# Attention over 64 groups of heads: first scores issued behind the second scores, two inversions and the output's addition reordered, constants made inside the first router

## The chip, the cores and the metric

One core of a Trainium2 chip runs the whole program in one launch. Its engines work side by side and meet at semaphores: TensorE (PE; its weight loads are shown as PEld), VectorE (DVE), ScalarE (ACT), GpSimd (POOL), and SyncE (SP), which issues most DMAs. The metric is the device time of one launch in microseconds (us).

## The reference, cut to what matters

Layers in a row, each with a layer norm ahead and a residual addition behind: a mixture of experts (a router, 64 experts, 8 chosen for each token, at most 128 tokens each), the gated linear attention that this change is about, a second mixture of experts, and a closing stage. The attention, per head (16 sequences of 256 tokens, 16 heads, 64 key, 64 slot and 128 value channels):

```
s = clip(x @ Ws, -32, 32);  z = cumlogsumexp(s over time)
g = exp(z shifted by one - z);  p = exp(s - z)
ok_t = q_t . hk_t     with hk_t = hk_(t-1) * g_t + k_t p_t       (first scan)
pv   = softmax(ok)
ov_t = pv_t . hv_t    with hv_t = hv_(t-1) * g_t + p_t v_t       (second scan)
out  = (rmsnorm(ov) * silu(x @ Wg)) @ Wo
```

## The kernel before

The program is a row of stages: router and experts (0 to about 325 us), attention (to about 1790 us), router and experts again, closing. Before the first router two short stages stand: `constants` lets GpSimd make the identity, the causal mask and a few index tables, and `attention_weights` lets SyncE issue two small loads. Each such stage ends in a meeting of all engines, and only then does the router's SyncE issue the loads of x.

**The scans as matrices.** Both scans are turned into masked matrix products over the 256 tokens (two tiles of 128). With e = exp(s) (`em`) and its running sum over time (`running_sum`, then `invert`, giving `rz` = 1/sum), the first scan is: scores k.q of tokens j <= t (`scores_a`), masked (`masked_first`, into `at`), times e (`slots_read`, into PSUM bank `psC[0]`), times `rz` (`okn`). The softmax weights times `rz` are `pzT`. The second scan is: scores e.pz (`scores_b`), masked (`masked_second`, into `bt`), times v (`over_j`, into `psD`), plus for the second tile the state of the first (`state_of_slots`, copied by ScalarE to `state`, read by `state_read`).

**Rounds.** Attention is a software pipeline of 64 rounds, N = 16 sequences x 4 groups of 4 heads (`QPB` = 4). In round n TensorE finishes group n and projects group n+1. Its order is written out by hand in the last loop of `attention`: value(n+1, first half), slots_read(n), state_of_slots(n), slots(n+1), turn_back(n), value(n+1, second half), query(n+1), turn_weights(n), turn_exps(n+1), turn_output(n-1), key(n+1), scores_b(n), state_read(n), gate(n+1) twice, over_j(n), output(n-1), scores_a(n+1). VectorE and ScalarE have orders of their own. In every fourth round a new sequence's normalised x is turned (`turn_stream`) between the two gates, and copied in two parts by ScalarE (`high_of_stream`) and VectorE (`low_of_stream`).

**Names in the rows.** A projection is three matmuls for each part (lines 1460 to 1462 of `split_matmul`). L1292 is scores_b, L1304 state_read, L1268 and L1271 are scores_a (256 and 128 columns), L1316 slots_read, L1279 state_of_slots, L1325 turn_back. Key and slot channels are 64, so the scores use half of the array's rows: the trace shows them as 64*128, two heads side by side, while projections are 128*128 and slots_read and state_of_slots are 128*64. Float32 products are two records for each matmul. On VectorE L1092 is masked_second, L1086 masked_first, L1109 the running sums, L1113 the inversions, L1102 the gated output, L1098 the gate, L1076 the output's addition, L1117 the squares, L1139 okn.

**PSUM.** `psA[0]` and `psA[1]` take turns for all projections. `first_banks` are the four banks into which scores_a writes: both of `psB`, `psC[1]` and one of `psD`. So scores_a has to wait until the masks, the exps' copy, the gated output and the squares have read these banks.

Of the kernel before, what the change touches and what calls it, by code (L numbers as in the profile page):

```python
# [17 lines left out]
ALU = mybir.AluOpType  # L18
# [19 lines left out]
EPS = 1e-5  # L38
ROW = D + E
# [53 lines left out]
def constants(nc, mem):  # L93
# [14 lines left out]
    with nc.Block(no_gpsimd_drain=True) as block:  # L108
        @block.gpsimd
        def _(pool):  # L110
            nc.gpsimd.memset(c["ident"][:, :], 0.0).then_inc(s_set, 1)
            nc.gpsimd.memset(c["causal"][:, :, :], 1.0).then_inc(s_set, 1)
            nc.gpsimd.memset(c["minus_half"][:, :], -0.5).then_inc(s_set, 1)
            pool.wait_ge(s_set, 3)
            nc.gpsimd.affine_select(out=c["ident"][:, :], in_=c["ident"][:, :], compare_op=ALU.not_equal,
                                    fill=1.0, base=0, pattern=[[-1, P]], channel_multiplier=1).then_inc(s_cut, 1)
            for blk in (0, 2):
                nc.gpsimd.affine_select(out=c["causal"][:, blk, :], in_=c["causal"][:, blk, :],
                                        compare_op=ALU.is_ge, fill=0.0, base=0, pattern=[[1, P]],
                                        channel_multiplier=-1).then_inc(s_cut, 1)  # L120
            nc.gpsimd.memset(c["earlier"][:, :], 0.0).then_inc(s_blocks, 1)
            pool.wait_ge(s_blocks, 1)
            for k in range(4):
                own = slice(32 * k, 32 * k + 32)
                nc.gpsimd.memset(c["earlier"][own, own], 1.0).then_inc(s_blocks, 1)
                nc.gpsimd.iota(base_i[own, :], pattern=[[0, 1]], base=1, channel_multiplier=P).then_inc(s_iota, 1)
            pool.wait_ge(s_blocks, 5)
            pool.wait_ge(s_iota, 4)
            nc.gpsimd.iota(row_i[:, :], pattern=[[1, P]], base=0, channel_multiplier=0).then_inc(s_iota, 1)
            nc.gpsimd.iota(col_i[:, :], pattern=[[0, 1]], base=0, channel_multiplier=1).then_inc(s_iota, 1)  # L130
            nc.gpsimd.affine_select(out=c["earlier"][:, :], in_=c["earlier"][:, :], compare_op=ALU.is_ge, fill=0.0,
                                    base=-1, pattern=[[1, P]], channel_multiplier=-1).then_inc(s_cut, 1)
            pool.wait_ge(s_iota, 6)
            nc.gpsimd.tensor_copy(c["slot_row"][:, :], row_i[:, :]).then_inc(s_cut, 1)
            nc.gpsimd.tensor_copy(c["slot_col"][:, :], col_i[:, :]).then_inc(s_cut, 1)
            nc.gpsimd.tensor_copy(c["tile_base"][:, :], base_i[:, :]).then_inc(s_cut, 1)
            pool.wait_ge(s_cut, 7)
            nc.gpsimd.tensor_scalar(c["slot_half"][:, :], c["slot_col"][:, :], 0.5, None, ALU.add).then_inc(s_cut, 1)
            nc.gpsimd.tensor_scalar(c["slot_pad"][:, :], c["slot_col"][:, :], float(NTOK - P + 1), None, ALU.add).then_inc(s_cut, 1)
            pool.wait_ge(s_cut, 9)  # L140
    return c


def moe_router(nc, cst, tag, past, x_src, gate_w, rows, fresh, slot_tok, behind=()):
# [10 lines left out]
    with ExitStack() as ctx:  # L155
# [79 lines left out]
        with nc.Block(no_gpsimd_drain=True) as block:  # L235
            @block.sync
            def _(sp):
# [16 lines left out]
                for j in range(1, NJ):  # L254
                    load(j)
                if fresh:
# [19 lines left out]
            def _(act):  # L276
# [14 lines left out]

                act.wait_ge(gw_turned, DC)
# [62 lines left out]
            def _(dve):  # L355
# [32 lines left out]

                for j in range(S):
                    moments_of(j)  # L390
# [57 lines left out]
            def _(pe):  # L448
# [25 lines left out]

                pe.wait_ge(gw_here, 16)
# [283 lines left out]
def attention_weights(nc, mem, g_norm, lut):  # L759


    w = {"norm": mem.sb("g_norm", [P, 1]), "lut": mem.sb("lut_row", [P, NLUT]), "here": mem.sem("attention_weights")}
    with nc.Block(no_gpsimd_drain=True) as block:
        @block.sync
        def _(sp):
            with nc.allow_non_contiguous_dma(reason="128 words, once"):
                sp.dma_start(w["norm"][:, :], g_norm.rearrange("(v o) -> v o", o=1)).then_inc(w["here"], 16)
            sp.dma_start(w["lut"][:, :], lut.partition_broadcast(P)).then_inc(w["here"], 16)
    return w


def attention(nc, cst, w, tag, past, stream_a, stream_b, x_out, second, zero_row, indices, looked_up):
# [10 lines left out]
    with ExitStack() as ctx:  # L783
# [16 lines left out]
        at = mem.sb("at", [P, HQ, 3 * P])  # L800
        bt = at.rearrange("p h i -> p (h i)")[:, 0:HQ * T].rearrange("p (q s i) -> p q s i", q=2, i=P)
        state = at.rearrange("p h i -> p (h i)")[:, HQ * T:HQ * T + NH * DV].rearrange("p (a v) -> p a v", a=NH)
        sq = mem.sb("sq", [P, TT * HQ * DV])
        okn = sq[:, 0:NH * T].rearrange("p (a t) -> p a t", a=NH)
# [18 lines left out]
        psO = [psD[:, k, :] for k in range(2)]  # L823
        first_banks = psB + [psC[1], psO[0]]
# [31 lines left out]
        with nc.Block(no_gpsimd_drain=True) as block:  # L856
# [186 lines left out]
            def _(dve):  # L1043
# [85 lines left out]
                for a in range(NH):  # L1129
                    invert(0, a)  # L1130
# [957 lines left out]
```

## Time and profile before

| | us |
|---|---|
| median of 3 runs | 2640.36 (2638.11 to 2642.53) |
| the profiled execution | 2640.57 |
| its span, first to last instruction | 2638.4 |
| TensorE busy | 2341.7 (89%) |
| VectorE busy | 1736.6 (66%) |
| GpSimd busy | 1241.8 (47%) |
| ScalarE busy | 886.0 (34%) |
| DMA, mean rate over the span | 63 GB/s |

By slices of the span, TensorE is 90% busy or more from about 400 us to 1780 us and again from 2200 us on: the attention and the closing stage. In the two router and expert stages it is 40 to 80% busy and the DMA engines carry 150 to 275 GB/s. The granted TensorE clock is full through attention and falls to half in stretches of the router and expert stages. A busy share says how full an engine is, not who is waited for: for that, the timeline of one round is read engine by engine.

### The profile page before, as it was taken

What the parts mean: (1) busy time and instruction counts of PE and PEld (TensorE: products, weight loads), DVE (VectorE), ACT (ScalarE), POOL (GpSimd) and SP (SyncE); (2) the same over time, 40 slices, a digit from 0 to 9 for tenths busy, and PEclk for the clock granted to TensorE, in tenths of its full rate; (3) what the DMA queues carried; (4) which work ended last, traced back from release to release, by engine and by line L of the source; (5) the groups of instructions that cost most, each with busy time, mean ns of one, the idle gap of its engine ahead of it and who ended that gap; (6) DMA issues with size and microseconds to landing.
All of it is one profiled execution on the core that took longest, in us unless ns stands there. A gap on an engine that the chain in (4) does not pass through costs nothing. (4 is left out here: it accounts for less than half of the span.)

```text
span 2638.4 us, 46098 instructions
## 1 busy us (share of the span) xinstructions
PE 2341.7 (89%) x18006; PEld 2076.9 (79%) x18006; DVE 1736.6 (66%) x3420; ACT 886.0 (34%) x1768; POOL 1241.8 (47%) x1214
## 2 busy tenths in 40 slices
PE   7656499999999999999999999987566489999998
PEld 7545388889899888989998889877554377888887
DVE  6433267888787788777887887766422266776654
ACT  5322133333333333333333333324322133333332
POOL 3477634555455555545554555452488521221111
PEclk9788799999999999999999999988799799999999
DMA  8989500000000000000000000004799500000000
GB/s 275 274 224 216 115 13 21 5 17 22 9 17 17 21 6 19 19 21 5 17 21 21 6 17 21 13 3 153 207 218 215 120 24 17 25 25 25 17 9 16
DMA packets 188230, 165.43 MB, mean 63 GB/s; under 512 B 28432, under 2 KB 180976, under 8 KB 187504
## 3 DMA queue, kind: packets, MB, share of 16 engines
q1 hardware_dynamic: 161072, 120.53, 14.9%
q0 software_dynamic: 24576, 37.77, 7.8%
q10 hardware_dynamic: 2368, 4.19, 0.5%
q8 instruction: 145, 2.38, 0.4%
q14 instruction: 69, 0.57, 0.1%
HBM read 115.84 MB, written 51.04 MB: 63 GB/s over the span
## 5 line engine op out<-in xcount | busy, mean ns | idle before, releaser
L947 POOL TENSOR_TENSOR a_orstd<-a_ms,minus_half 128x8 f32<-128x8 f32 x64 | 106.7, 1667 | 467.6 <-DVE a_ms L1120 467.6
L927 POOL TENSOR_SCALAR a_pick<-a_index,lut_row 128x258 f32<-128x258 int32 x240 | 280.8, 1170 | 24.3
L1113 DVE RECIPROCAL a_rz<-a_rz 128x256 f32<-128x256 f32 x128 | 215.6, 1716 | 0.0
L630 PE MATMUL e_psX<-ident,e_xg 128*128 128x128 f32 x256 | 61.7, 327 | 167.3 <-DMA e_xg<-rows,slot_tok 166.7
L746 DVE TENSOR_TENSOR e_hT<-e_psH,e_sil 128x128 f32<-128x128 f32 x128 | 37.2, 291 | 256.5 <-ACT e_sil L704 151.7
L630 PEld LDWEIGHTS e_psX<-ident,e_xg 128*128 128x128 f32 x256 | 30.7, 156 | 211.9 <-DMA e_xg<-rows,slot_tok 208.6
L930 POOL TENSOR_TENSOR a_found<-a_found,a_pick 128x258 f32<-128x258 f32 x240 | 177.4, 739 | 20.0
L600 POOL DMA_INDIRECT e_xg<-rows,slot_tok x128 | 129.9, 1015 | 93.5 <-POOLq L235 55.1
L958 ACT ACTIVATE a_v<-a_psA 128x512 f32<-128x512 f32 x128 | 76.5, 598 | 224.1 <-PE a_psA L1462 224.1
L1460 PE MATMUL a_psC<-wo_high,a_oT 128*128 128x256 f32 x512 | 150.2, 293 | 1.5 <-DVE a_oT L1066 1.5
L1460 PE MATMUL f_pair<-f_lnT,wguT 128*128 128x512 f32 (+1 forms) x352 | 143.7, 408 | 7.5 <-DVE f_lnT L1726 7.2
L1461 PE MATMUL a_psC<-wo_low,a_oT 128*128 128x256 f32 x512 | 144.6, 282 | 0.0
L1462 PE MATMUL a_psC<-wo_high,a_oT 128*128 128x256 f32 x512 | 144.4, 282 | 0.0
L1737 DVE TENSOR_TENSOR f_hs<-f_pair,f_sil 128x512 f32<-128x512 f32 x96 | 66.1, 689 | 117.0 <-PE f_pair L1462 106.8
L1461 PE MATMUL f_pair<-f_lnT,wguT 128*128 128x512 f32 (+1 forms) x352 | 140.9, 400 | 0.0
L1462 PE MATMUL f_pair<-f_lnT,wguT 128*128 128x512 f32 (+1 forms) x352 | 140.6, 400 | 0.0
L952 POOL TENSOR_TENSOR a_o<-a_o,a_orstd 128x512 f32<-128x512 f32 x128 | 131.0, 1044 | 5.0
L1036 ACT ACTIVATE a_sq<-a_psD 128x512 f32<-128x512 f32 x128 | 76.6, 598 | 165.0 <-DVE a_o L1102 98.0
L1343 PEld LDWEIGHTS a_psD<-a_v,a_at 128*128 128x128 f32 x1024 | 124.2, 192 | 5.9 <-DVE a_at L1092 0.2
L1634 ACT ACTIVATE f_sil<-f_pair 128x512 f32<-128x512 f32 x96 | 57.2, 597 | 211.0 <-PE f_pair L1462 211.0
L688 ACT ACTIVATE e_xgT<-e_psX 128x256 f32<-128x256 f32 x128 | 49.0, 383 | 232.0 <-PE e_psX L630 195.6
L1092 DVE TENSOR_TENSOR a_at<-a_psB,causal 128x512 f32<-128x512 f32 x128 | 82.5, 686 | 65.2 <-PE a_psB L1292 65.2
(279 smaller groups left out, 7857.3 us busy)
## 6 DMA issues: line engine op xcount, KB each, us to landing
e_wg<-in_L_ffn_w_gate SPq DMA_DIRECT2D x128, 128.0 KB
e_wu<-in_L_ffn_w_up SPq DMA_DIRECT2D x128, 128.0 KB
e_wd<-in_L_ffn_w_down SPq DMA_DIRECT2D x128, 128.0 KB
rows<-r_row SPq DMA_DIRECT2D x32, 320.0 KB, 2.8
stream_b<-r_zeros SPq DMA_DIRECT2D x11, 384.0 KB, 4.9
stream_c<-rows SPq DMA_DIRECT2D x33, 128.0 KB, 3.2
r_xt<-in_L_attn_hidden_states SPq DMA_DIRECT2D x16, 256.0 KB, 5.6
stream_a<-r_xt SPq DMA_DIRECT2D x16, 256.0 KB, 3.6
```

Of the source, the lines that this page charges most:

```text
L600: pool.indirect_dma_start(out=xg[:, e % U, :], out_offset=None, in_=rows, in_offset=bass.IndirectOffsetOnAxis(ap=slot_tok[:, e:e + 1], axi ...
L630: nc.tensor.transpose(psX[u][:, c, :], xg[:, e % U, c * P:(c + 1) * P], cst["ident"][:, :]).then_inc(turned[u], 1)
L927: nc.gpsimd.tensor_scalar(pick[:, :, :], index[:, :, :], float(c), w["lut"][:, c:c + 1], ALU.is_equal, ALU.mult).then_inc(picked, 1)
L930: nc.gpsimd.tensor_tensor(out=found[:, :, :], in0=found[:, :, :], in1=pick[:, :, :], op=ALU.add).then_inc(looked, 1)
L947: nc.gpsimd.tensor_tensor(out=flat(orstd[:, :, :]), in0=ms[:, :], in1=cst["minus_half"][:, 0:TT * HQ], op=ALU.pow).then_inc(orstd_ok, 1)
L952: nc.gpsimd.tensor_tensor(out=part, in0=part, in1=orstd[:, :, 2 * a:2 * a + 2].unsqueeze(3).to_broadcast([P, TT, 2, DV]), op=ALU.mult).the ...
L1092: nc.vector.tensor_tensor(out=bt[:, p, :, :], in0=psB[p].rearrange("p (s i) -> p s i", i=P), in1=cst["causal"][:, 0, :].unsqueeze(1).to_br ...
L1113: nc.vector.reciprocal(rz[:, a, :], rz[:, a, :]).then_inc(rz_ok, 1)
L1343: mm = nc.tensor.matmul(psD[:, p, (t * NH + a) * DV:(t * NH + a + 1) * DV], bt[:, p, a * TT + t, :], v[:, n % 2, t, h * DV:(h + 1) * DV], ...
L1460: nc.tensor.matmul(out, lhs[0], rhs[0], start=first, stop=False)
L1461: nc.tensor.matmul(out, lhs[0], rhs[1], start=False, stop=False)
L1462: return nc.tensor.matmul(out, lhs[1], rhs[0], start=False, stop=last)
```

## The change

**Scores.** scores_a is split. `own_scores`, shared with scores_b, makes the products of each token tile with itself (8 matmuls of 128 columns, into the two `psA` banks that query and key have just left), and `scores_below` makes those of the first tile with the second (4 matmuls of 128 columns, into the first half of `psD`). The below part needs no mask: ScalarE copies it (`below_copy`, two copies of 128x256) into a new tile `below`, whose first half is `state` at other times. VectorE masks the own part with two operations of 128x512 instead of four of 128x384. `bt` now lies in `sq`. All of it stands right behind scores_b(n). The first projection of value(n+1) now comes behind slots_read and state_of_slots, output(n-1) comes ahead of over_j, the gates behind it. The gates wait for the masks of the first scores. `turn_stream` writes `psB[1]`, and low_of_stream comes behind the gates on VectorE. over_j signals once, not once for each bank, and waits for the below copies.

```diff
-                def masked_first(m):
-                    for h in range(HQ):
-                        dve.wait_ge(at_ps, HQ * m + h + 1)
-                        nc.vector.tensor_tensor(out=at[:, h, :], in0=first_banks[h][:, 0:3 * P],
...
+                def masked_first(m):
+                    masked(at, [psA[1 - m % 2], psA[m % 2]], m, at_ps, at_ok)
...
+                def below_copy(m):
+                    act.wait_ge(below_ps, m + 1)
+                    for p in range(2):
+                        copy(flat(below[:, p, :, :]), psD[:, p, 0:NH * P], below_ok)
...
                 def gate(m, t):
-                    if t == 0:
-                        pe.wait_ge(q_ok, m + 1)
-                    else:
-                        pe.wait_ge(k_ok, m + 1)
+                    pe.wait_ge(at_ok, 2 * m + t + 1)
...
                 def scores_a(m):
                     pe.wait_ge(k_ok, m + 1)
                     pe.wait_ge(q_ok, m + 1)
-                    pe.wait_ge(et_ok, m + 1)
-                    if m > 0:
-                        pe.wait_ge(bt_ok, 2 * m)
...
+                    own_scores(kT, qT, [psA[1 - m % 2], psA[m % 2]], at_ps)
+
+                def scores_below(m):
+                    if m > 1:
+                        pe.wait_ge(otl_ok, NH * (m - 1))
...
                 def slots_read(n):
+                    pe.wait_ge(at_ok, 2 * n + 2)
+                    pe.wait_ge(below_ok, 2 * n + 2)
...
                 def over_j(n):
+                    if n + 1 < N:
+                        pe.wait_ge(below_ok, 2 * n + 4)
```

On TensorE, in a third round, this stands in a row where scores_a was and where it is now (the names are output<-inputs; a_ stands for attention). Before:

```order
L1462 MATMUL a_psC<-wo_high,a_oT 128x256
L1268 MATMUL a_psB<-a_qT,a_kT 128x256 x2
L1271 MATMUL a_psB<-a_qT,a_kT 128x128 x2
L1268 MATMUL a_psC<-a_qT,a_kT 128x256
L1268 MATMUL a_psD<-a_qT,a_kT 128x256
L1271 MATMUL a_psC<-a_qT,a_kT 128x128
L1271 MATMUL a_psD<-a_qT,a_kT 128x128
L1460 MATMUL a_psA<-wv_high,a_lnT 128x512
```

Now, behind the last matmul of key and ahead of the first of output:

```order
L1479 MATMUL a_psA<-a_lnT,wk_low 128x256
L1269 MATMUL a_psB<-a_pzT,a_emT 128x128 x8
L1269 MATMUL a_psA<-a_qT,a_kT 128x128 x8
L1287 MATMUL a_psD<-a_qT,a_kT 128x128 x4
L1315 MATMUL a_psD<-a_below,a_pzT 128x128 x4
L1477 MATMUL a_psC<-wo_high,a_oT 128x256
```

All products of 64 channels are one run, and between two runs of that shape no projection is left in which they would have to be set up again.

**VectorE's order.** masked_first(n+1) moves right behind masked_second(n), the inversions stay behind the sums, and add_output(n-1) moves from behind the gates to between the two inversions. Before, on VectorE in the same round:

```order
L1092 TENSOR_TENSOR a_at<-a_psB,causal 128x512 x2
L1109 SCALAR_TENSOR_TENSOR a_rz<-causal,a_psC 128x256 x2
L1113 RECIPROCAL a_rz<-a_rz 128x256 x2
L1102 TENSOR_TENSOR a_o<-a_psD,a_tg 128x4x128 x2
L1098 SCALAR_TENSOR_TENSOR a_tg<-a_tg,a_psA 128x512 x2
L1076 TENSOR_TENSOR a_xacc<-a_psC,a_xacc 128x512
L1086 TENSOR_TENSOR a_at<-a_psB,causal 128x384 x2
L1086 TENSOR_TENSOR a_at<-a_psC,causal 128x384
L1086 TENSOR_TENSOR a_at<-a_psD,causal 128x384
L1117 TENSOR_REDUCE a_ss<-a_sq 128x8
```

Now:

```order
L1097 TENSOR_TENSOR a_sq<-a_psB,causal 128x512 x2
L1097 TENSOR_TENSOR a_at<-a_psA,causal 128x512 x2
L1120 SCALAR_TENSOR_TENSOR a_rz<-causal,a_psC 128x256 x2
L1124 RECIPROCAL a_rz<-a_rz 128x256
L1087 TENSOR_TENSOR a_xacc<-a_psC,a_xacc 128x512
L1124 RECIPROCAL a_rz<-a_rz 128x256
L1113 TENSOR_TENSOR a_o<-a_psD,a_tg 128x4x128 x2
L1109 SCALAR_TENSOR_TENSOR a_tg<-a_tg,a_psA 128x512 x2
L1128 TENSOR_REDUCE a_ss<-a_sq 128x8
```

The mask of the first scores has left the place ahead of the squares; the same holds ahead of the first round, with one difference, that there the two inversions stand ahead of the mask.

**Start.** The stage `constants` is gone: its GpSimd work runs at the head of the router's GpSimd program, and VectorE, ScalarE and TensorE wait there for its nine last operations. The stage `attention_weights` is gone: SyncE issues its two loads behind the 16 loads of x.

```diff
+def moe_router(nc, cst, tag, past, x_src, gate_w, rows, fresh, slot_tok, behind=(), make=None, late=()):
...
                 for j in range(1, NJ):
                     load(j)
+                for dst, src, here in late:
...
+                act.wait_ge(cst["made"], MADE)
...
                 past.clear(pool)
+                if make:
+                    make(pool)
...
+                dve.wait_ge(cst["made"], MADE)
                 for j in range(S):
                     moments_of(j)
...
+                pe.wait_ge(cst["made"], MADE)
                 pe.wait_ge(gw_here, 16)
```

SyncE's program began before with:

```order
L764 UNCONDITIONAL_BRANCH
L767 DMA g_norm<-in_L_attn_g_norm_weight 128x1
L768 DMA lut_row<-in_L_ffn_lut 128x16
L763 UNCONDITIONAL_BRANCH
L236 UNCONDITIONAL_BRANCH
L240 DMA r_xt<-in_L_attn_hidden_states 128x2x256 x2
```

and begins now with:

```order
L238 UNCONDITIONAL_BRANCH
L242 DMA r_xt<-in_L_attn_hidden_states 128x2x256 x2
L255 DMA r_gw_in<-in_L_ffn_gate_w 64x256
L242 DMA r_xt<-in_L_attn_hidden_states 128x2x256 x14
L260 DMA g_norm<-in_L_attn_g_norm_weight 128x1
L260 DMA lut_row<-in_L_ffn_lut 128x16
```

The loads of x are now the first thing on SyncE, with no meeting of the engines ahead of them.

## Rows read from the trace of the kernel before

**Rows 1.** Windows, the attention stage: busy us of each engine, then TensorE's clock share.

```profile
327.00:1780.00 1453.00, 1438.73 (x12324) 1295.06 (x12324) 1146.42 (x1769) 515.56 (x912) 754.58 (x747) 0.99 0.05 15
```

**Rows 2.** Timeline, PE, round at 1004 us: start us, us, line, operation, shape, count.

```profile
1003.84 1.16 PE L1292 MATMUL a_psB<-a_pzT,a_emT 64*128 64x128 f32 x16
1004.83 0.61 PE L1304 MATMUL a_psD<-a_at,a_pzT 64*128 64x128 f32 x8
...
1012.68 0.28 PE L1461 MATMUL a_psC<-wo_low,a_oT 128*128 128x256 f32 x1
1012.79 0.28 PE L1462 MATMUL a_psC<-wo_high,a_oT 128*128 128x256 f32 x1
1013.00 0.70 PE L1268 MATMUL a_psB<-a_qT,a_kT 64*128 64x256 f32 x4
...
1013.98 0.38 PE L1268 MATMUL a_psC<-a_qT,a_kT 64*128 64x256 f32 x1
...
1014.19 0.27 PE L1271 MATMUL a_psC<-a_qT,a_kT 64*128 64x128 f32 x1
...
1014.30 0.27 PE L1271 MATMUL a_psC<-a_qT,a_kT 64*128 64x128 f32 x1
...
1014.51 0.51 PE L1460 MATMUL a_psA<-wv_high,a_lnT 128*128 128x512 f32 x1
1014.85 0.40 PE L1461 MATMUL a_psA<-wv_low,a_lnT 128*128 128x512 f32 x1
1015.09 0.40 PE L1462 MATMUL a_psA<-wv_high,a_lnT 128*128 128x512 f32 x1
...
1019.54 0.60 PE L1325 MATMUL a_psC<-ident,a_sq 128*128 128x128 f32 x4
...
1026.07 1.16 PE L1292 MATMUL a_psB<-a_pzT,a_emT 64*128 64x128 f32 x16
```

**Rows 3.** Timeline, PE, the same operation at the end of a fourth round.

```profile
1049.08 1.16 PE L1292 MATMUL a_psB<-a_pzT,a_emT 64*128 64x128 f32 x16
```

**Rows 4.** Timeline, DVE, the same round.

```profile
1005.03 1.29 DVE L1092 TENSOR_TENSOR a_at<-a_psB,causal 128x512 f32<-128x512 f32 x2 [0.94 <-PE a_psB L1292]
...
1014.35 1.01 DVE L1086 TENSOR_TENSOR a_at<-a_psB,causal 128x384 f32<-128x384 f32 x2
...
1016.21 1.21 DVE L1117 TENSOR_REDUCE a_ss<-a_sq 128x8 f32<-128x1024 f32 x1
...
1017.69 0.69 DVE L1139 TENSOR_TENSOR a_sq<-a_psC,a_rz 128x512 f32<-128x512 f32 x1
```

**Rows 5.** Timeline, ACT, the same round: the copy of the keys.

```profile
1003.94 0.60 ACT L958 ACTIVATE a_kT<-a_psA 128x512 f32<-128x512 f32 x1 [0.78 <-PE a_psA L1462]
```

**Rows 6.** Timeline, all engines, the start of the program.

```profile
5.23 0.21 POOL L139 TENSOR_SCALAR slot_pad<-slot_col 128x1 f32<-128x1 f32 x1
...
7.20 0.89 SPq L240 DMA_DIRECT2D r_xt<-in_L_attn_hidden_states  x2
...
10.77 1.41 DVE L361 BATCH_NORM_STATS2 r_bs<-r_xt 128x6 f32<-128x256 f32 x4 [10.77 <-DMA r_xt<-in_L_attn_hidden_states]
...
14.03 1.40 DVE L361 BATCH_NORM_STATS2 r_bs<-r_xt 128x6 f32<-128x256 f32 x4 [1.44 <-DMA r_xt<-in_L_attn_hidden_states]
```

**Rows 7.** Timeline, all engines, ahead of attention's first round.

```profile
339.32 3.34 DVE L1113 RECIPROCAL a_rz<-a_rz 128x256 f32<-128x256 f32 x2
...
344.93 1.66 PE L1316 MATMUL a_psC<-a_at,a_em 128*64 128x128 f32 x24
```

**Rows 8.** Timeline, PE, in the first experts: a wait of 2.66 us.

```profile
227.62 0.64 PE L630 MATMUL e_psX<-ident,e_xg 128*128 128x128 f32 x2 [2.66 <-DMA e_xg<-rows,slot_tok]
```

**Rows 9.** Windows, right behind that wait (columns as in Rows 1).

```profile
227.80:231.00 3.20, 3.20 (x14) 2.78 (x14) 0.43 (x2) 1.38 (x3) 2.59 (x3) 0.50 0.89 182
```

**Rows 10.** Timeline, DVE, attention's last round.

```profile
1769.08 1.29 DVE L1102 TENSOR_TENSOR a_o<-a_psD,a_tg 128x512 f32<-128x512 f32 x2 [1.66 <-PE a_psD L1343]
...
1772.54 1.21 DVE L1117 TENSOR_REDUCE a_ss<-a_sq 128x8 f32<-128x1024 f32 x1
```

More of the change, by code:

```diff
@@ L38 @@
 EPS = 1e-5
+MADE = 9
 ROW = D + E
@@ L107, in constants @@
     s_set, s_cut, s_blocks, s_iota = mem.sem("c_set"), mem.sem("c_cut"), mem.sem("c_blocks"), mem.sem("c_iota")
[L108 to L140, printed above, removed]
@@ L1253, in turn_exps, with own_scores @@
                     mm.then_inc(et_ps, 1)
+                def own_scores(lhs, rhs, banks, ready):
+                    for a in range(NH):
+                        for t in range(TT):
+                            for p in range(2):
+                                r, own = p * DK, slice(t * P, (t + 1) * P)
+                                mm = nc.tensor.matmul(banks[p][:, (a * TT + t) * P:(a * TT + t + 1) * P], lhs[r:r + DK, a, own], rhs[r:r + DK, a, own],
+                                                      start=True, stop=True)
+                                if a == NH - 1 and t == TT - 1:
+                                    mm.then_inc(ready, 1)
                 def scores_a(m):
@@ L1287, in scores_b, with state_read @@
                     pe.wait_ge(st_ok, n + 1)
[L1288 to L1297 removed]
+                    pe.wait_ge(lnTl_ok, n // QPB + 1)
+                    own_scores(emT, pzT, psB, bt_ps)
+                def state_read(n, more):
                     if n > 0:
@@ L1371, in _ @@
                 turn_exps(0)
+                scores_a(0)
+                scores_below(0)
                 gate(0, 0)
                 gate(0, 1)
-                scores_a(0)
                 for n in range(N):
                     ahead = n + 1 < N
-                    if ahead:
-                        value(n + 1, 0)
                     slots_read(n)
@@ L1394, in _ @@
                     scores_b(n)
-                    state_read(n)
+                    if ahead:
+                        scores_a(n + 1)
+                        scores_below(n + 1)
+                    state_read(n, ahead)
+                    if n > 0:
+                        output(n - 1)
+                    over_j(n)
                     if ahead:
@@ L1400, in _ @@
                         gate(n + 1, 1)
-                    over_j(n)
-                    if n > 0:
-                        pe.wait_ge(lnTl_ok, min((n + 1) // QPB + (2 if (n + 1) % QPB == QPB - 1 else 1), B))
-                        output(n - 1)
-                    if ahead:
-                        scores_a(n + 1)
                 turn_output(N - 1)
```

149 lines of the change are left out of this document (84 added, 65 removed).

## The prediction

> **What bounds the kernel now.** I read the page by slices first: the attention stage is more than half of the span, and TensorE is full in it. The windows view puts a number on it: of 1453 us of attention TensorE works 1438.73 at full clock (0.99), VectorE 1146, ScalarE 516, GpSimd 755 [rows 1]. So a round costs what TensorE's row of matmuls costs, and a change pays if it shortens that row. The timeline of TensorE through one round is next. The round from one scores_b to the next is 1026.07 - 1003.84 = 22.23 us, a fourth round 1049.08 - 1026.07 = 23.01 us [rows 2, 3]. Inside it TensorE is never without work, but steps between matmuls are not even: output's matmuls follow each other in 0.12 us, the last one holds 0.21 before scores_a starts (1012.79 to 1013.00); within scores_a a pass of two heads takes 0.21 for 256 columns (1013.98 to 1014.19) and 0.11 for 128 (1014.19 to 1014.30), but its last pass of 128 again holds 0.21 (1014.30 to 1014.51); value's first matmul then takes 0.34 where the next takes 0.24 [rows 2]. The longer steps stand where the shape changes from 128*128 to 64*128 and back. That is what the change takes out.
>
> **The round's matmuls, part by part.** scores_a takes 1014.51 - 1013.00 = 1.51 us [rows 2]. Its columns alone are four passes of 256 and four of 128 for pairs of heads: 4 x 0.215 + 4 x 0.107 = 1.29 us. Moved into the run behind scores_b, it is eight passes of 128 (own) and four (below), 12 x 0.107 = 1.29 us again: the columns are the same. state_read follows scores_b today with no long step between them (16 records, 1003.84 to 1004.83, 0.99 us, are eight passes and one step of 0.11-0.14 at the run's start) [rows 2], so I price the joints inside the new run at nothing. What goes: 1.51 - 1.29 = 0.22 in scores_a, 0.21 - 0.12 = 0.09 ahead of it, 0.34 - 0.24 = 0.10 behind it: 0.41 us. The other shape changes stay in number: the run ends into output instead of the gate, the gate instead of value goes into slots_read (128*64), state_of_slots goes into value instead of slots. Six changes become four, and I take 0.40 us a round. Bounds: 0.19, if the 0.22 inside scores_a belongs to its waits and not to the shape, and 0.50, if a pair's start is also saved.
>
> The change has 12 matmuls where 8 stood. The row shows no price for that: half the columns take half the time, 0.11 against 0.21 [rows 2]. The Trainium skill (TensorEngine Tiling, Instruction Overhead) gives each matmul about 60 cycles of overhead; by it, as an estimate, four more matmuls of two passes at 2.4 GHz would cost 0.2 us a round and leave half of the gain, 12 us less in all. The row decides for no price.
>
> 62 of the 63 rounds that look ahead gain this: 62 x 0.40 = 24.8 us.
>
> **Which waits could take it back.** In the new order, counted from scores_b's start: scores_a needs the keys' copy. ScalarE begins it at 1003.94 and ends it 0.70 behind scores_b's start [rows 2, 5], scores_a is due at 0.99: 0.3 to spare. Its banks psA are left by then. scores_below (due at 1.85) needs low_of_output, which was ready for state_read. The run ends at 2.83. Output has no new wait. over_j needs the below copies: ScalarE can start them at 2.9; a copy of 128x512 is 0.60 [rows 5], so two of half the size are at most 1.2, done by 4.1; over_j is due behind output's 24 matmuls, at 5.75. The gates (7.45) need the masks, done at about 3.7. Queued behind ScalarE's below copies are turned_exps and the squares, due later still.
>
> VectorE is the engine to watch, since okn and turn_back hang on it. Today it goes from masked_second (1005.03) to okn (1017.69) in 12.66 us [rows 4]. The four masks of 128x384 there take 1016.21 - 1014.35 = 1.86; two masks of 128x512 take what masked_second takes, about 1.21. Everything else is the same work in another order. So okn starts 12.0 us behind masked_second, at 1.19 + 12.0 = 13.2, and is done at 13.9. turn_back stands today at 1019.54 - 1003.84 = 15.70 [rows 2], and would stand at 15.3. VectorE is 1.4 us ahead. The addition between the inversions waits for output (ended at 5.8), the second inversion ends at 8.6, over_j's single signal comes at 7.7: no wait. GpSimd's output scaling starts with the squares, 0.5 earlier than today, like its user. Earlier stores of the addition only help the next sequence's accumulator.
>
> In the fourth rounds value(n+2) waits for low_of_stream, which now stands behind the gate on VectorE: ScalarE's second tanh 11.6, high part 12.1, low part 12.95, value due at 12.8: 0.2 to 0.3 us of wait. Today these rounds cost 0.78 more than others [rows 2, 3], of which the turn is 0.43 (four transposes, 0.36, and a step of 0.07 at the gate behind them); new: 0.43 + 0.27 = 0.70. 15 x 0.08 = 1.2, I take 1.0 us gained.
>
> **Ahead of the first round** the change loses. VectorE inverts twice before it masks: the inversions run from 339.32 to 342.6 [rows 7]. The gates now wait for these masks (343.3), where they filled this time before; TensorE, whose new scores are done 1.4 us behind the keys' copy, near 339.8, stands until 343.3, 3.5 us. Then gates (3.0) and slots_read at 346.3, where it was at 344.93 [rows 7], and value(1) (1.5) still follows: 1.4 + 1.5 = 2.9, less 0.1 for a shape step: 2.8 us lost. A pause of 2.66 us in the experts was followed by 3.2 us at half clock (0.50) [rows 8, 9]; that would cost 1.7 here. It need not happen; I take 1.0, bounds 0 and 3.4.
>
> **Behind the last round** output(62) now runs ahead of over_j(63). The gated output moves from 1769.08 to about 1771.9; then square and second part, and the squares' sum starts near 1773.0 instead of 1772.54 [rows 10]: 0.5 lost. The last turn before it waits for VectorE and gains about the 0.5 of okn: together nothing.
>
> **Start.** GpSimd's constants end at 5.44 and are not touched in length; the loads of x are issued at 7.20, and VectorE starts on them at 10.77, 3.57 later; on the second batch at 14.03 [rows 6]. In the new order SyncE issues them as its first work, which I put at 0.8 (the constants' own stage, about 4.6 us long, cannot have begun later than that), so they are there at 4.4, and VectorE starts when the constants are made, 5.5: 5.3 earlier. The second batch is there at 7.6, 6.4 earlier. What follows hangs on both, and all later stages shift with it; the two late small loads add 0.8 us to SyncE ahead of its zero stores, which nobody waits for. I take 6.0, bounds 4 (part of it swallowed by busy DMA engines in the experts) and 6.4.
>
> **Sum** against the profiled execution, 2640.57, which is the median (2640.36) within 0.2: - 24.8 (rounds) - 1.0 (fourth rounds) + 2.8 + 1.0 (before the first) + 0 (end) - 6.0 (start) = - 28.0, 2612.6; I say 2612.
>
> **Rivals.**
> A, part of the joint is not saved: the long steps are scores_a's own waits, and the joint of scores_b and scores_a, with new operands and a wait on the keys' copy 0.3 us away, costs as much again. Then 0.19 a round, 62 x 0.21 = 13 us less: 2625. For it: two semaphores stand ahead of scores_a; against it, state_read follows scores_b without a step, though it waits too.
> B, slower: the loop over VectorE becomes the bound. Its work from masked_second to okn is in series with turn_back, two projections, the exps and scores_b. It has 1.4 us to spare of the new round, so 1.4 + 0.40 = 1.8 us against today's. It turns slower only where the new order puts more than 1.9 us of waits into VectorE's row, as if over_j's one late signal, the two tanh and the inversions fell in series instead of overlapping. At 2.1 us: 63 x 0.3 = 19 us slower than now, with - 6 + 3.8 at the edges, 2657. The ends worked out above speak against it: the signal comes 0.9 ahead of its reader.
> C, the start saves nothing, because the DMA-bound experts set the time: 2618; inside the range.
> D, the waits of several tenths spread over the round eat the gain just so far that nothing is measured: 2640.
>
> **How the numbers follow.** Forecast (2603 to 2621, C's case within) 0.77; A (to 2632) 0.13; lower than 2603, a larger saving at the joints, 0.03; B 0.05; D 0.02. A measurement of this kernel can tell about 0.2%, 5 us, from no change. Faster 0.93, same 0.02, slower 0.05. The range takes the bounds of the start (2 us), of the clock (2.4) and a good part of A: 2602 to 2628.
>
> **What would show it.** TensorE's timeline: L1269, L1269, L1287, L1315 in one run of about 2.83 us, and rounds of 21.84 (fourth rounds 22.5). The first x statistics at 5.5 us. One new wait of TensorE of about 3.5 us at the first gates, in the first round a short wait of over_j and value. If the round is 22.0 or more, the waits of TensorE name which semaphore; if it is PEld that starts late at the second L1269, it is A. If VectorE's okn ends behind the last slots matmul, it is B.

## The result

| | before | after |
|---|---|---|
| median of 4 runs, us | 2641.23 (2638.11 to 2642.53) | 2611.10 (2609.42 to 2613.99) |
| the profiled execution, us | 2640.57 | 2609.42 |
| its span, us | 2638.4 | 2607.7 |

The ratio is 0.9892, with a 95% interval of 0.9880 to 0.9903: 28.5 us faster by the ratio, 30.8 by the two profiled spans. The forecast was 2612.

The page of the changed kernel: span, then busy us of each engine with its share and instructions.

```profile
span 2607.7 us, 47039 instructions
PE 2317.5 (89%) x18518; PEld 2077.7 (80%) x18518; DVE 1691.2 (65%) x3292; ACT 927.1 (36%) x1896; POOL 1241.8 (48%) x1214
```

TensorE is busy 24 us less, in the same share of the span, and ScalarE 41 us more, which are the below copies. Attention by windows, as in [rows 1]: TensorE is still full and its clock still whole.

```profile
311.00:1750.00 1439.00, 1414.37 (x12840) 1294.15 (x12840) 1102.45 (x1646) 556.58 (x1041) 760.09 (x752) 0.99 0.06 15
```

**The round.** TensorE's timeline, over the same operations as [rows 2, 3]: the end of key, the joined run, the start of output, and scores_b one round before and one and two rounds later.

```profile
987.97 0.38 PE L1269 MATMUL a_psB<-a_pzT,a_emT 64*128 64x128 f32 x2
...
1009.64 0.28 PE L1479 MATMUL a_psA<-a_lnT,wk_low 128*128 128x256 f32 x1
1009.85 1.16 PE L1269 MATMUL a_psB<-a_pzT,a_emT 64*128 64x128 f32 x16
1010.85 1.06 PE L1269 MATMUL a_psA<-a_qT,a_kT 64*128 64x128 f32 x16
1011.74 0.61 PE L1287 MATMUL a_psD<-a_qT,a_kT 64*128 64x128 f32 x8
1012.19 0.61 PE L1315 MATMUL a_psD<-a_below,a_pzT 64*128 64x128 f32 x8
1012.73 0.38 PE L1477 MATMUL a_psC<-wo_high,a_oT 128*128 128x256 f32 x1
...
1032.41 1.16 PE L1269 MATMUL a_psB<-a_pzT,a_emT 64*128 64x128 f32 x16
...
1054.29 0.38 PE L1269 MATMUL a_psB<-a_pzT,a_emT 64*128 64x128 f32 x2
```

The four blocks of 64*128 follow each other with no wait: scores_b holds TensorE for 1010.85 - 1009.85 = 1.00 us, the own scores 0.89, the below scores 0.45, state_read 0.54 up to output. The run takes 2.88 us. Ordinary rounds are 1009.85 - 987.97 = 21.88 and 1054.29 - 1032.41 = 21.88 us long, where they were 22.23; the fourth round between them is 22.56, where it was 23.01.

**Where the 30.8 us are.** The same landmarks on both traces, by the start of TensorE's operation, and of VectorE's last addition for attention's last operation (us from the span's start; the gains are taken before rounding):

| landmark | before | after | gained in this piece |
|---|---|---|---|
| first matmul of the first expert | 88.8 | 83.8 | 5.1 |
| attention's first turn | 325.2 | 317.2 | 2.9 |
| first scores_b | 354.1 | 350.4 | -4.2 |
| scores_b of round 1 | 375.4 | 370.6 | 1.0 |
| scores_b of round 62 | 1744.0 | 1715.5 | 23.8 |
| last scores_b | 1764.0 | 1734.5 | 1.0 |
| attention's last operation | 1785.2 | 1756.6 | -0.9 |
| closing's first turn | 2098.2 | 2069.3 | 0.2 |
| end of the span | 2638.4 | 2607.7 | 1.9 |

Attention itself is 24 us of it, the start 5, and 3 + 2 us came in stages whose instructions are the same in both kernels. Of the 24.8 us from the first scores_b to that of round 62, round 0 gives 1.0 (21.21 us before, 20.18 now), the 61 rounds behind it 0.36 each (22.24 to 21.88 us in the mean of the 46 ordinary ones), and the 15 fourth rounds among these 1.9 more.

**Ahead of the first round** the forecast wait is there. All engines, with the wait in brackets:

```profile
330.28 3.34 DVE L1124 RECIPROCAL a_rz<-a_rz 128x256 f32<-128x256 f32 x2
...
333.54 1.22 DVE L1097 TENSOR_TENSOR a_at<-a_psA,causal 128x512 f32<-128x512 f32 x2
...
334.22 0.80 PE L1477 MATMUL a_psA<-wg_high,a_lnT 128*128 128x512 f32 x1 [3.30 <-DVE a_at L1097]
```

VectorE inverts from 330.28 to 333.5 and masks only then; TensorE's first gate stands 3.30 us for that mask. Behind it the windows view (busy us of PE, PEld, DVE, ACT, POOL, then the clock) shows TensorE at 0.50 for 6.4 us:

```profile
333.60:340.00 6.40, 5.78 (x16) 4.16 (x18) 1.85 (x4) 0.85 (x2) 0.00 (x0) 0.50 0.00 0
```

By narrower windows the stretch at half clock runs from 333.4 to 340.2. Against it stands the half-clock stretch of attention's own start, just before: 306.2 to 333.5 in the kernel before and 299.3 to 323.2 now. TensorE does nothing in it until the first turn; from there on it is 8.3 us in the kernel before (325.2 to 333.5) and 6.0 us now (317.2 to 323.2).

**VectorE in the round** goes through masks, sums, inversions and addition in one row, as [rows 4] did in another order:

```profile
1011.05 1.29 DVE L1097 TENSOR_TENSOR a_sq<-a_psB,causal 128x512 f32<-128x512 f32 x2 [1.03 <-PE a_psB L1269]
1012.25 1.28 DVE L1097 TENSOR_TENSOR a_at<-a_psA,causal 128x512 f32<-128x512 f32 x2
...
1014.62 1.73 DVE L1124 RECIPROCAL a_rz<-a_rz 128x256 f32<-128x256 f32 x1
...
1024.13 0.69 DVE L1150 TENSOR_TENSOR a_sq<-a_psC,a_rz 128x512 f32<-128x512 f32 x1
...
1025.89 0.60 PE L1340 MATMUL a_psC<-ident,a_sq 128*128 128x128 f32 x4
```

okn (L1150) ends at 1024.82 here, turn_back (L1340) starts 1.07 later, in this fourth round; in ordinary rounds it is 1.42, and 1.06 in some of those just ahead of a fourth round. The one wait of TensorE that is new inside the rounds, by the view of waits (what waited, for whom: us in total, times, longest us):

```profile
PE a_psA L1477 <- DVE a_lnT L1071: 2.6, 15, 0.2
```

That is value(n+2) waiting for low_of_stream, once in each of 15 fourth rounds.

**The start.** All engines; SPq is SyncE's issue:

```profile
0.79 0.94 SPq L242 DMA_DIRECT2D r_xt<-in_L_attn_hidden_states  x2
...
5.48 1.41 DVE L369 BATCH_NORM_STATS2 r_bs<-r_xt 128x6 f32<-128x256 f32 x4 [5.48 <-POOL slot_pad L139]
...
7.23 1.41 DVE L369 BATCH_NORM_STATS2 r_bs<-r_xt 128x6 f32<-128x256 f32 x4
```

The loads go out at 0.79 instead of 7.20, VectorE starts its statistics at 5.48 instead of 10.77, behind the last constant and no longer behind a DMA, and does the second batch at 7.23 instead of 14.03 [rows 6].

### The profile page after: what moved, and what is told of

It reads as the page before. It is cut to its first block and busy times, and to the rows that moved or that the text cites. A ratio compares the mean times of both kernels' runs of the same rounds, so it can differ in the third digit from the quotient of the medians.

```text
span 2607.7 us, 47039 instructions
## 1 busy us (share of the span) xinstructions
PE 2317.5 (89%) x18518; PEld 2077.7 (80%) x18518; DVE 1691.2 (65%) x3292; ACT 927.1 (36%) x1896; POOL 1241.8 (48%) x1214
## 5 line engine op out<-in xcount | busy, mean ns | idle before, releaser
L1124 DVE RECIPROCAL a_rz<-a_rz 128x256 f32<-128x256 f32 x128 | 221.4, 1731 | 0.0
L1109 DVE SCALAR_TENSOR_TENSOR a_tg<-a_tg,a_psA 128x512 f32<-128x512 f32 x128 | 87.9, 688 | 61.1 <-ACT a_tg L1005 55.3
L1360 PE MATMUL a_psD<-a_v,a_sq 128*128 128x128 f32 x1024 | 124.8, 275 | 0.8 <-ACT a_below L962 0.8
```

The source lines that it names most:

```text
L1109: nc.vector.scalar_tensor_tensor(out=tg[:, t, :], in0=tg[:, t, :], scalar=1.0, in1=psA[(1 - m % 2) if t == 0 else m % 2], op0=ALU.add, op1 ...
L1124: nc.vector.reciprocal(rz[:, a, :], rz[:, a, :]).then_inc(rz_ok, 1)
L1360: mm = nc.tensor.matmul(psD[:, p, (t * NH + a) * DV:(t * NH + a + 1) * DV], bt[:, p, a * TT + t, :], v[:, n % 2, t, h * DV:(h + 1) * DV], ...
```

## The experiments

The theories that they tell apart: a round gains by the two changes of array shape that are gone (the forecast), or by scores_a's waits that are gone (rival A); VectorE's loop has 1.2 to 1.4 us of room, and decides the sign beyond it (rival B); the earlier start reaches the end of the program or is swallowed by the DMA-bound experts (rival C). All ratios are against runs of the kernel before on the same chip.

### start_alone and attention_alone: the two parts apart

`start_alone` is the changed kernel with its whole `attention` as in the kernel before; in the row of a round:

```diff
-                    if ahead:
-                        scores_a(n + 1)
-                        scores_below(n + 1)
-                    state_read(n, ahead)
-                    if n > 0:
-                        output(n - 1)
-                    over_j(n)
+                    state_read(n)
...
+                    over_j(n)
...
+                        output(n - 1)
+                    if ahead:
+                        scores_a(n + 1)
```

> The kernel before with the start's part of the change alone (constants made at the head of the router, no stage for the two small loads). Theory: the first statistics start at 5.5 us instead of 10.8, the first experts' first matmul about 5 us earlier, and later stages shift along: 2635 (2633 to 2637). Rival C: the DMA-bound experts set the time and swallow it: 2641, with attention starting where it did, at 325 us.

Measured: 2630.51 us (2628.49 to 2632.20) against 2637.64 (2633.50 to 2639.61), ratio 0.9973 (0.9963 to 0.9984), 7.1 us faster. `attention_alone` is the other half, the kernel before with the changed `attention`, so the same lines the other way round:

> The kernel before with the attention's part of the change alone; constants and the two small loads stay in stages of their own. Theory: rounds - 24.8, ahead of the first round + 4.2, the end 0, as in the changed kernel's trace: about - 21 us, a ratio of 0.992 to the kernel before (2616 where before is 2637), and from the first experts' first matmul to attention's start between 233 and 238 us, wherever the start stands. If the experts' stage is 3 us shorter only when the program starts earlier, this kernel shows 236 and the others 233.

Measured: 2619.13 us (2613.68 to 2621.20) against 2639.44 (2635.88 to 2643.93), ratio 0.9917 (0.9898 to 0.9936), 22 us faster, with rounds of 21.88 us. The ratios multiply to 0.9890, the whole change has 0.9892: the parts add. Rival C has fallen.

The view of one tile (line, engine, tile and count: least, median and longest ns, from first to last us) gives the experts' first and attention's first matmul. Of start_alone, then of attention_alone:

```profile
L640 PE MATMUL e_psX<-ident,e_xg x128: 272/328/476, 82.5 to 290.0; 128*128 128x128 f32 x128
L1200 PE MATMUL a_psC<-ident,a_xab x4: 421/421/473, 315.6 to 316.3; 128*128 128x128 f32 x4
```

```profile
L630 PE MATMUL e_psX<-ident,e_xg x128: 272/328/476, 89.6 to 297.6; 128*128 128x128 f32 x128
L1201 PE MATMUL a_psB<-ident,a_xab x4: 421/421/476, 323.2 to 323.9; 128*128 128x128 f32 x4
```

The first matmul of the experts comes 6.3 us earlier with the new start (88.8 before) and 0.8 later without it. In the nine traces that have the new start it stands at 82.2 to 83.8, in the mean 83.1, in the two without it at 88.8 and 89.6: 6.1 us between the means. From there to attention it takes 315.6 - 82.5 = 233.1 with the new start and 323.2 - 89.6 = 233.6 without it, 236.3 in the trace of before, 233.5 in that of after, and 231.9 to 237.6 over all eleven traces of this study. So the 2.9 us that the experts gave on top are their scatter from one execution to another, not the change.

### turn_between and turn_behind: is it the shape?

Each adds one turn of the identity (128*128, into a bank that output is about to overwrite), the first inside the joined run, the second at its end, where the shape changes anyway. The work added is the same; only the first adds two shape changes.

```diff
                     scores_b(n)
+                    nc.tensor.transpose(psC[0][:, 0:P], ident, ident)
                     if ahead:
                         scores_a(n + 1)
```

```diff
                     state_read(n, ahead)
+                    nc.tensor.transpose(psC[0][:, 0:P], ident, ident)
```

> The same turn, but between scores_b and scores_a, so that the run of 64*128 products is cut in two. Nothing else moves and no wait is added. Theory (the saving is the change of shape): 0.09 for the turn and the 0.36 us a round that the change gained come back: 63 x 0.45 = 28 us over the changed kernel, 2639, scores_b's block grows by about 0.3 us and scores_a's by 0.1. Rival A (the saving lies in fewer or earlier waits): the same as the control, 2617.

> The changed kernel plus one turn of the identity (128*128, 128 columns) in each round, behind state_read and ahead of output, where the shape changes anyway. Both theories: 0.09 us a round for the turn itself and no new change of shape: 63 x 0.09 = 6 us, 2617. It is the control for the next kernel.

turn_between took 2637.55 us (2632.95 to 2640.07), ratio 1.0000 (0.9991 to 1.0010): the whole gain of attention and of the start is gone. turn_behind took 2612.81 (2609.80 to 2614.47), ratio 0.9901 (0.9884 to 0.9917), as the change itself. TensorE's timeline of turn_between:

```profile
1045.13 1.16 PE L1269 MATMUL a_psB<-a_pzT,a_emT 64*128 64x128 f32 x16
1046.22 0.33 PE L1412 MATMUL a_psC<-ident 128*128 128x128 f32 x1
1046.48 1.16 PE L1269 MATMUL a_psA<-a_qT,a_kT 64*128 64x128 f32 x16
1047.47 0.61 PE L1287 MATMUL a_psD<-a_qT,a_kT 64*128 64x128 f32 x8
```

and of turn_behind:

```profile
1015.59 0.61 PE L1287 MATMUL a_psD<-a_qT,a_kT 64*128 64x128 f32 x8
1016.03 0.61 PE L1315 MATMUL a_psD<-a_below,a_pzT 64*128 64x128 f32 x8
1016.58 0.33 PE L1416 MATMUL a_psC<-ident 128*128 128x128 f32 x1
1016.66 0.36 PE L1478 MATMUL a_psC<-wo_high,a_oT 128*128 128x256 f32 x1
```

In the run, scores_b holds TensorE for 1.09 us instead of 1.00, the turn for 1046.48 - 1046.22 = 0.26, the own scores for 0.99 instead of 0.89. At the end of the run the same turn holds 1016.66 - 1016.58 = 0.08, and output's first matmul is 0.05 shorter for it, since the change of shape is now paid ahead of it. Rounds are 22.30 and 21.91 us: the two shape changes cost 0.39 us, which over 63 rounds is the 24.7 us between the two medians. In both kernels the semaphores and their order are the same, so rival A's waits have no part in it. The Trainium skill (TensorEngine Tiling (Array Packing), Key Properties) says that a change of tiling mode drains TensorE; the 0.39 us agrees in kind, and the page gives no size.

### vector_sums_1 and vector_sums_2: how much room VectorE has

Behind masked_first(n+1) VectorE sums a tile that is ready, once or twice; nobody uses the result. The edit for two sums:

```diff
                         masked_first(n + 1)
+                        dve.wait_ge(tg_ok, TT * n + TT)
+                        if n > 0:
+                            dve.wait_ge(spared, 2 * n)
+                        for k in range(2):
+                            nc.vector.reduce_sum(spare[:, k:k + 1], flat(tg[:, :, :]), axis=AX.X).then_inc(spared, 1)
```

> The changed kernel with one more sum of 128x1024 (about 1.2 us, its result unused) in VectorE's row of each round, behind the masks of the first scores. Theory: VectorE is 1.4 us ahead at turn_back and 1.2 at value's first half, so the ordinary rounds do not move by more than 0.1 us; in the 15 fourth rounds, where TensorE waits for low_of_stream already, the whole 1.2 shows: 15 x 1.2 = 18 us over the changed kernel, up to 24: 2629 to 2635. If VectorE had no room (rival B nearly true), 62 x 1.2 = 74: 2685. If it had much more room than thought, 2611.

> The same with two such sums, 2.4 us. Theory: room of 1.2 us used up, so 1.2 in each of 48 ordinary rounds and 2.4 in 15 fourth rounds, 58 + 36 = 94 us over the changed kernel, 2705: slower than the kernel before, as rival B said for waits of over 1.9 us. If the room is nearer 2 us: 2640 to 2660.

VectorE's timeline of vector_sums_1 shows the sum behind the masks and the running sums behind it:

```profile
1013.71 1.28 DVE L1099 TENSOR_TENSOR a_at<-a_psA,causal 128x512 f32<-128x512 f32 x2
1014.90 1.21 DVE L1180 TENSOR_REDUCE a_spare<-a_tg 128x1 f32<-128x1024 f32 x1
1016.03 1.25 DVE L1122 TENSOR_TENSOR_SCAN a_rz<-causal,a_psC 128x256 f32<-128x256 f32 x2
```

It holds VectorE for 1016.03 - 1014.90 = 1.13 us. vector_sums_1 took 2622.92 us (2616.26 to 2625.48) against 2636.37 (2635.15 to 2649.14), ratio 0.9947 (0.9926 to 0.9968). Its ordinary rounds are 21.89 us in the mean, 0.01 longer than without the sum; its fourth rounds 23.03, 0.47 longer, and less than the 1.2 that I had expected. The view of waits has the reason: there TensorE waits for VectorE's low_of_stream, and in the changed kernel VectorE stands idle for 0.56 us ahead of the second gate, just before it, so part of the sum was covered.

```profile
PE a_psA L1484 <- DVE a_lnT L1073: 9.7, 15, 0.7
```

From the first to the last scores_b this kernel takes 10 us more than the change, where 18 to 24 were expected. By the two ratios (0.9947 and 0.9892) it is 14.5 us; the traced execution was the fastest of the four. vector_sums_2, one run, took 2696.18 us. Ordinary rounds are 23.03 us, longer by 1.15, as expected, fourth rounds 24.15. The view of waits, from 400 to 1700 us, has 42 rounds in which the first matmul of a projection waits for VectorE to leave its bank (a_tg is the gate's product), and the 14 fourth rounds as before:

```profile
PE a_psA L1484 <- DVE a_tg L1111: 46.0, 42, 1.1
PE a_psA L1484 <- DVE a_lnT L1073: 24.9, 14, 1.8
```

In ordinary rounds the first sum costs 0.01 us, and both cost 1.15, so the room is 2 x 1.13 - 1.15 = 1.1 us. That is a little less than the 1.4 that the prediction had read at turn_back: the gate's bank is due first (1.22 us to spare in the changed kernel's trace). With two sums the kernel is 60 us slower than the one before (2636.37). Rival B's mechanism is real, its point lies 0.3 us nearer than forecast, and the change doesn't reach it.

### addition_back: the output's addition behind the gates, as it was

```diff
                         invert(n + 1, 0)
-                    if n > 0:
-                        add_output(n - 1)
                     if ahead:
                         invert(n + 1, 1)
...
                             low_of_stream((n + 1) // QPB + 1)
+                    if n > 0:
+                        add_output(n - 1)
                     squares(n)
```

> The changed kernel with the output's addition back behind the gates on VectorE, where it stood before. slots_read of the next round waits for it, since both use the bank psC 0. It would be done about 12.5 us behind scores_b's start, and slots_read is due at 10.45: 2.1 us a round, 62 x 2.1 = 130 us over the changed kernel, 2741. Rival (the move of the addition was free, VectorE has room): 2611.

One run: 2767.97 us, where the kernel before takes 2636.37 on the same chip. From the first scores_b to that of round 62 it is 158 us more than the changed kernel. The timeline of PE and DVE in an ordinary round, and the view of waits:

```profile
1024.50 0.68 DVE L1087 TENSOR_TENSOR a_xacc<-a_psC,a_xacc 128x512 f32<-128x512 f32 x1
1025.24 0.44 PE L1331 MATMUL a_psC<-a_at,a_em 128*64 128x128 f32 x4 [2.07 <-DVE a_xacc L1087]
```

```profile
PE a_psC L1331 <- DVE a_xacc L1087: 131.1, 59, 2.7
```

slots_read writes the bank that the addition reads, so TensorE stands 2.07 us in each ordinary round and 2.67 in a fourth: the rounds are 24.0 and 25.05 us. In the kernel before, scores_a and value stood between the gates and slots_read and gave the addition its time; now only the gates and over_j lie between output and slots_read. So the joined run pays only with this move beside it. The 130 us that I expected are this wait. The rest is clock: in 14 of the 61 rounds from round 1 to 61 TensorE fell to half clock within 1.4 us behind the end of this wait, for 3.4 us each, and such a round is 1.6 us longer, 25.6 us if ordinary and 26.6 if a fourth; 14 x 1.6 = 22 us. Ten of the 14 are fourth rounds, with the wait of 2.67 us, of which there are 15; four are ordinary, with 2.07 us, of which there are 46. In vector_sums_2, where TensorE waits 1.8 us in a fourth round and 1.1 in an ordinary one, it is two of 15 and none of 46. So in these two kernels the half clock follows more often the longer the wait is. One such stretch and what follows it, by windows:

```profile
1099.80:1103.00 3.20, 3.20 (x15) 2.43 (x12) 0.69 (x1) 0.00 (x0) 3.12 (x3) 0.50 0.00 0
1103.20:1106.00 2.80, 2.80 (x22) 2.62 (x21) 1.07 (x2) 1.21 (x3) 2.52 (x4) 1.00 0.00 0
```

### mask_ahead and both_edges: the two ends mended

`mask_ahead` lets VectorE mask the first round's scores before it inverts:

```diff
+                masked_first(0)
                 for a in range(NH):
                     invert(0, a)
-                masked_first(0)
                 gate(0, 0)
```

> The changed kernel with the first scores' masks ahead of the two inversions on VectorE before round 0 only. Theory: TensorE's pause of 3.3 us at the first gates goes, and with it the stretch of half clock of 6.8 us that follows it (3 us): the first scores_b comes 5 to 6 us earlier, 2605 to 2606. If the half clock has another cause, 2608. Rival (okn's inversions then hold TensorE as long as the masks did): 2611.

It took 2606.11 us (2604.80 to 2608.76), ratio 0.9882 (0.9865 to 0.9898). PE and DVE:

```profile
331.65 1.29 DVE L1097 TENSOR_TENSOR a_at<-a_psA,causal 128x512 f32<-128x512 f32 x2
332.39 0.50 PE L1477 MATMUL a_psA<-wg_high,a_lnT 128*128 128x512 f32 x1 [0.33 <-DVE a_at L1097]
332.86 3.35 DVE L1124 RECIPROCAL a_rz<-a_rz 128x256 f32<-128x256 f32 x2
...
345.89 1.16 PE L1269 MATMUL a_psB<-a_pzT,a_emT 64*128 64x128 f32 x16
```

The wait of 3.30 us is 0.33, and the gates and what follows run at full clock, by windows:

```profile
331.00:340.00 9.00, 8.67 (x80) 7.22 (x77) 6.80 (x8) 3.22 (x7) 0.00 (x0) 1.00 0.01 2
```

From the first turn to the first scores_b it takes 28.7 us, as in the kernel before (29.0), where the change takes 33.1. The other traces agree: seven have the wait of 3.30 us, and a stretch of half clock begins within a microsecond of its end in all seven, 6.8 us long in two (the change and vector_sums_1) and 3.4 in five. The four without this wait have no such stretch.

`both_edges` has this, and in the last round over_j stands ahead of output again, and add_output(62) behind the gated output:

```diff
-                    if n > 0:
+                    if n > 0 and ahead:
                         add_output(n - 1)
...
                     gated_output(n, 0)
+                    if not ahead:
+                        add_output(n - 1)
...
                     state_read(n, ahead)
+                    if not ahead:
+                        over_j(n)
                     if n > 0:
                         output(n - 1)
-                    over_j(n)
+                    if ahead:
+                        over_j(n)
```

> The changed kernel with the masks of the first scores ahead of the two inversions before round 0, and, in the last round alone, over_j ahead of output and the output's addition behind the gated output, as they stood before the change. Theory: 4 to 5 us from the first, 0.5 to 0.9 us from the second: 0.9868 to 0.988 of the kernel before, 2605.5 on the chip of the first timing. If the last round's order costs nothing, the same as with the masks alone.

It took 2604.99 us (2602.79 to 2614.89) against 2636.37, ratio 0.9881 (0.9861 to 0.9901). From the last scores_b to the squares' means it takes 9.34 us instead of 9.91, so the order at the end is worth some 0.5 us in the trace. start_alone and attention_alone, the old order and the new, compare better, since neither has more than 0.1 us of half clock behind its last scores_b: 8.88 and 9.64 us, 0.76 between them. In the time it can't be seen. Both kernels come out ahead of the change (0.9892), but all three intervals overlap: a better version is likely, and not proven by the times. The 4.5 us in the trace of mask_ahead are the firmest part of it.

## Why the prediction was right

**The round.** Forecast 0.40 us, measured 0.36 in the mean of 46 ordinary rounds. The cause is the one named, two of six shape changes less: put back, they cost 0.39. The two steps inside scores_a, of which the text was not sure, stood at its ends, next to the other shape. The last is in [rows 2]; for the first, from the same timeline of the kernel before:

```profile
1013.00 0.70 PE L1268 MATMUL a_psB<-a_qT,a_kT 64*128 64x256 f32 x4
1013.54 0.39 PE L1271 MATMUL a_psB<-a_qT,a_kT 64*128 64x128 f32 x4
```

Two passes of 256 columns take 0.54 us here, where one alone takes 0.21 further on in [rows 2]: 0.11 too much.

What is missing is in the term for the new run, 2.83 us forecast and 2.88 measured. The twelve passes of the first scores take 0.89 + 0.45 = 1.34 us, 0.112 each, where I had 1.29 from 0.107 each. So a pass of 128 columns costs 0.004 more than half of one with 256 (0.216). The four matmuls more are 0.03 us of the 0.05; the rest is that the four passes of 128 that stood in scores_a before were put too low as well. The Trainium skill (TensorEngine Tiling (Array Packing), Instruction Overhead) puts about 60 cycles on each matmul, from which the prediction worked out an estimate of 0.2 us; the rows show 0.03. From the first scores_b to that of round 62, which are 62 rounds, the landmarks show 1.0 + 23.8 = 24.8 us gained; forecast for them, fourth rounds included, were 24.8 + 1.0 = 25.8.

**Fourth rounds.** In the mean of 15 their excess over an ordinary round was 0.81 us and is 0.68, where 0.70 was forecast, with the wait for low_of_stream at 0.17 us against 0.27. They give 15 x 0.13 = 1.9 us against 1.0. Round 0 gives 0.7 us more than an ordinary round, which was not in the sum. So a part of what the ordinary rounds lack came from terms that were put too low or not at all.

**The waits.** In ordinary rounds none of the limits that the text went through ends last. ScalarE copies the below scores late enough to be seen and early enough not to matter:

```profile
1009.96 0.60 ACT L962 ACTIVATE a_kT<-a_psA 128x512 f32<-128x512 f32 x1 [0.78 <-PE a_psA L1479]
...
1012.85 0.66 ACT L962 ACTIVATE a_below<-a_psD 128x256 f32<-128x256 f32 x2 [2.29 <-PE a_psD L1315]
```

The keys' copy starts 0.11 us behind scores_b and ends 0.29 ahead of the own scores, with 0.3 forecast. The below copies start 3.00 us behind scores_b (2.9 forecast). VectorE is 1.42 us ahead at turn_back, with 1.4 forecast; what was missed is that the gate's bank is due with less to spare, 1.2 (and turn_back itself with 1.06 in some rounds), and the sums show 1.1.

**Ahead of the first round.** Forecast +2.8 and +1.0 for the clock, measured +4.2, against +3.8; the pause is 3.30 against 3.5 us. The prediction said that the half clock need not happen and took 1.0 for it; it came in all seven traces that have the pause. In the one behind this result it is 6.8 us long, twice the length of [rows 9]. That it cost little more than forecast is luck in part: from its first turn on, attention's opening had 2.3 us less of half clock. mask_ahead takes 4.5 us of it back.

**Behind the last round.** Forecast 0, measured +1.0 for the last turn and -0.9 from the last scores_b to the end. The loss was forecast at 0.5, from the order of output and over_j, and the gain at 0.5. start_alone and attention_alone, with the clock alike, show these two sizes: the step from the scores_b of round 62 to the last is 20.03 and 19.57 us, 0.46 gained, with 3.4 us of half clock in both, and the order loses 0.76. In the two profiled executions the clock adds the rest. The last turn has 3.7 us of half clock in the kernel before and 1.6 in the change. Up to the squares' means the change loses only 9.91 - 9.76 = 0.15, since the kernel before stands at half clock for the first 3.1 us of that piece and the change for 1.8. The last output then takes 4.76 and 5.50 us, because the half-clock stretch over it ends 1.0 us before its end in the kernel before and covers all of it in the change. So the zero came out by the clock as well as by the argument.

**The start.** Forecast 6.0; 5.1 to the first expert in the profiled execution, 6.3 in start_alone's and 7.1 (4.2 to 9.8 by its interval) in its times, and 6.1 between the means of the traces with and without the new start. The bound of 6.4 was the second batch of x; its statistics came 14.03 - 7.23 = 6.8 us earlier, because VectorE no longer waits for it at all. It is inside the range, and no closer, since the experts scatter by some us.

**Not forecast and not explained by the change:** 2.9 us in the experts, which is their scatter, and 1.9 us in the closing stage, 540.3 against 538.4 us. No experiment addressed the closing stage, but its instructions are the same in all eleven traces and it takes from 538.4 to 544.3 us in them, so this too lies within its scatter. Without these 4.8 us the profiled execution would have been 1.6 us above the sum of 2612.6. So the total is closer than the terms deserve.

The rivals: A, which said 0.19 us a round, fell by the 0.36 and by turn_between against turn_behind, C by start_alone, B holds as a mechanism and needs more than 1.1 us on VectorE, and D has nothing to stand on, since TensorE's one wait that is new in the rounds comes to 2.6 us in all.

## What to carry to other kernels

Where TensorE is full, look at the steps between its blocks in the timeline: at each change between products over half of the array's rows and whole ones there is a step, and blocks of one shape that can stand together should, if their inputs are ready and their banks free. Then read the engine that follows TensorE for its slack, and confirm it by adding work that nobody uses, one dose at a time: the dose at which the round starts to grow is the room. A reordered pipeline has to be read at its edges too: the steady state's order (mask behind inversions) was the wrong one ahead of the first round, and a small addition left where it was would have cost 158 us, through the one PSUM bank that it reads, six times what the joined run gives.

## What the runs showed of the hardware

- A change between 64*128 and 128*128 and back costs 0.39 us, and it lies on the blocks at both sides: scores_b +0.09, own scores +0.10, and the turn 0.26 instead of 0.08.
- The same turn at a place where the shape changes anyway costs 0.03 us of the round.
- A pass over two heads side by side (64*128, one record of each) takes 0.112 us for 128 columns and 0.216 for 256 at full clock: four more, shorter matmuls for the same columns cost 0.03 us.
- At attention's first gates and in its rounds 1 to 61, half clock followed TensorE's waits the more often the longer they were: behind 3.30 us in 7 of 7 (for 3.4 or 6.8 us), behind 2.67 in 10 of 15, behind 2.07 in 4 of 46, behind 1.8 in 2 of 15, behind 1.1 in none of 46, and behind 0.33 in none of 2. A stretch of 3.4 us costs a round 1.6 us. Which of the waits of 2.07 to 2.67 us are followed by it stays open. One of 2.66 in the experts was, by 3.4 us [rows 8, 9].
- The stage of the experts, with the same instructions, took from 231.9 to 237.6 us from one execution to another, and the closing stage from 538.4 to 544.3. Of a gain of 5 us ahead of such a stage, a single trace can't tell at its end whether it arrived.
